# Differential attention with a gated feed-forward: branch-major order, and matmul work placed in pieces beside the scores

## The chip, the cores and the metric

One core of one Trainium2 chip runs the whole layer as one program. The metric is the device time in microseconds of an execution; smaller is better.

## The reference, cut to what matters

```python
x = L0_attn_x                       # (1, 1024, 256) float32
xn = layernorm(x)                   # no scale, no bias
# attention: 16 heads, two branches of queries and keys with 8 columns each, one set of values with 16
q1, k1, q2, k2, v = split(xn @ Wqkv, [128, 256, 384, 512])
lam = exp(lambda_q1 . lambda_k1) - exp(lambda_q2 . lambda_k2) + LAMBDA_INIT
A1 = causal_softmax(q1 k1^T / sqrt(8)) v
A2 = causal_softmax(q2 k2^T / sqrt(8)) v
diff = A1 - lam * A2
diff = (1 - LAMBDA_INIT) * diff / sqrt(mean(diff^2) + 1e-5)      # over the 16 columns of a head
attn = concat_heads(diff) @ Wproj
# feed-forward in fp8: 256 -> 2 x 1024 -> 256
ffn = (gelu(xn @ w_gating[0]) * (xn @ w_gating[1])) @ w_linear   # operands rounded to e4m3
out = x + attn + ffn
```

## The kernel before, in words

The program is written engine by engine, and each engine's list of instructions is its order; semaphores join them. There is no planner: the order of TensorE's work around the attention is written out by hand.

**Sizes.** 1024 tokens are eight blocks of 128 (TB). A group is four heads (J) of one branch; there are eight groups, and group g is heads g // 2 in branch g % 2, so the branches alternate. The causal scores of a head are cut into nine chunks of up to 512 columns (`CHUNKS`, line 42: key block, number of query blocks, first query); four heads times nine chunks are 36 items. A unit is three items, three of the eight PSUM banks: 12 units per group, 96 in all. Banks 0 to 2 and 3 to 5 hold the scores in turn; banks 6 and 7 collect the values' product, one for each half of the queries.

**Prefix.** VectorE normalizes x, TensorE transposes it (line 569), ScalarE copies it out. Eight units of queries and keys (line 584; `QK_UNITS` gives part and half, branch 1 is the first four) each go through ScalarE (high part, line 337) and VectorE (rest, line 419); SyncE spreads them by DMA over the partitions, eight DMAs for the stack of a group (line 228; four stacks fit, a later group's is loaded when an earlier group's scores are done). POOL squares the high parts (line 292). TensorE then projects the values (line 591), sums the squares into norms (line 603), makes 16 up products of the feed-forward (line 619), each followed by gelu on ScalarE (line 351) and the product with the second half on VectorE (line 436), and the down product (line 627), which VectorE copies out (line 445). From the norms VectorE works out a bound (line 368): a flag says whether exponentials could overflow without the row maxima, and a shift is the bias of the exponential. SyncE, VectorE and TensorE read the flag and run one of two bodies. With these inputs it is the one without row maxima.

**Attention.** Step n of the loop of TensorE (line 709) issues the scores of unit n (line 673), which wait for the exponential of unit n - 2, and then the values' product of the chunks that are due (line 695): chunk c of group g in step 12 g + last_unit(c) + `LAG`, with LAG = 3. ScalarE makes one exponential of 1536 columns per unit (line 360). POOL sets the part above the diagonal to zero in five of the nine chunks (line 319). The probabilities lie in a ring of six chunks (`KEPT`). When a half of the queries is complete, VectorE transposes it out of its bank (line 491), divides by the row sums (line 498), and after branch 2 of the same heads takes the difference, its mean square (lines 502 to 507), a root by bit shift and three Newton steps (lines 524 to 529; for the last heads by ScalarE's square root) and scales (line 511). A transpose back (line 544 or 549) makes the operand of the output projection (line 704), to which VectorE adds x and the feed-forward (line 556). Five DMAs write the output.

## Time and profile before

| what | value |
| --- | --- |
| median of 3 runs | 215.93 us (214.27 to 216.73) |
| the profiled execution | 216.52 us |
| its span | 214.7 us |
| busy: TensorE / ScalarE / VectorE / POOL | 181.4 / 162.7 / 92.2 / 62.3 us |
| granted TensorE clock, mean over the span | 0.971 |
| first exponential | 58.84 us |
| DMA, moved in all | 14.97 MB |

How to read it: the span is from the first to the last instruction of the profiled execution, and the execution's own time is 1.8 us longer. Busy time is a sum over the span; the stages have different limits, so what counts in each is which wait ends last. "PE" is TensorE (PEld its weight loads), "ACT" ScalarE, "DVE" VectorE, "POOL" GpSimd, "SP" SyncE. A clock of 1.00 is 2.4 GHz and 0.50 is 1.2 GHz. In the rows a time stands first (start in us), then the length in us, then engine, line, operation, output and input, and the count; brackets show how long the engine had idled and what ended that.

### The profile page before, as it was taken

What the parts mean: (1) busy time and instruction counts of PE and PEld (TensorE: products, weight loads), DVE (VectorE), ACT (ScalarE), POOL (GpSimd) and SP (SyncE); (2) the same over time, 40 slices, a digit from 0 to 9 for tenths busy, and PEclk for the clock granted to TensorE, in tenths of its full rate; (3) what the DMA queues carried; (4) which work ended last, traced back from release to release, by engine and by line L of the source; (5) the groups of instructions that cost most, each with busy time, mean ns of one, the idle gap of its engine ahead of it and who ended that gap; (6) DMA issues with size and microseconds to landing.
All of it is one profiled execution on the core that took longest, in us unless ns stands there. A gap on an engine that the chain in (4) does not pass through costs nothing.

```text
span 214.7 us, 3429 instructions
## 1 busy us (share of the span) xinstructions
PE 181.4 (84%) x1419; PEld 79.2 (37%) x1420; DVE 92.2 (43%) x182; ACT 162.7 (76%) x141; POOL 62.3 (29%) x71
## 2 busy tenths in 40 slices
PE   7699999997959988888888988888888888889970
PEld 7444485445722323322322332332232322232550
DVE  2835489885400004013961210992400595205581
ACT  2214334775096899999999999999999999999400
POOL 8306682000644203402601520440440350250000
PEclk9999999999975799999999999999999999999997
DMA  6965558840000034016007006100000000000014
GB/s 210 399 214 158 143 149 197 194 105 0 3 5 0 3 82 114 3 40 157 0 8 186 8 0 155 44 0 0 3 0 0 5 0 0 3 0 3 0 62 140
DMA packets 8149, 14.97 MB, mean 70 GB/s; under 512 B 1985, under 2 KB 5313, under 8 KB 8129
## 3 DMA queue, kind: packets, MB, share of 16 engines
q1 hardware_dynamic: 7584, 14.18, 24.0%
q10 hardware_dynamic: 544, 0.52, 0.7%
q8 instruction: 13, 0.21, 0.4%
q14 instruction: 8, 0.06, 0.1%
HBM read 5.26 MB, written 1.05 MB: 29 GB/s over the span
## 4 chain that ended last, share of the span: by engine, by line
ACT 62%; PE 29%; DVE 4%; DMA 2%; issue 1%; DVEq 0%; ACTq 0%
ACT probs L360 61%; PE ps L584 7%; PE ps L619 6%; PE ps L627 3%; PE ps L591 3%; PE ps L695 3%; PE ps L704 2%; PE ps L673 2%; DMA x_sb<-L_attn_x 2%; PE ps L569 1%; PE ps L603 1%; DVE stats L393 1%; DVE area L491 0%; DVE squares L544 0%; DVE area L436 0%
## 5 line engine op out<-in xcount | busy, mean ns | idle before, releaser
L360 ACT ACTIVATE probs<-ps,shift 128x1536 f32<-128x1536 f32 x96 | 137.9, 1853 | 10.0 <-PE ps L673 10.0
L695 PE MATMUL ps<-probs,v_all 128*32 128x512 f32 (+3 forms) x768 | 79.4, 510 | 0.4 <-ACT probs L360 0.4
L673 PE MATMUL ps<-q_st,k_st 32*128 32x512 f32 (+3 forms) x384 | 51.2, 432 | 21.3 <-ACT probs L360 20.9
L319 POOL TENSOR_SCALAR_AFFINE_SELECT probs<-probs 128x1024 f32<-128x1024 f32 (+1 forms) x40 | 38.0, 951 | 95.4 <-ACT probs L360 95.4
L673 PEld LDWEIGHTS ps<-q_st,k_st 32*128 32x128 f32 x384 | 23.4, 189 | 82.1 <-ACT probs L360 70.5
L491 DVE STREAM_TRANSPOSE area<-ps 128x512 f32<-128x512 f32 x16 | 11.4, 714 | 92.2 <-PE ps L695 92.1
L695 PEld LDWEIGHTS ps<-probs,v_all 128*32 128x32 f32 x768 | 17.2, 110 | 19.1 <-issue 13.7
L584 PE MATMUL ps<-xn_t,probs 128*128 128x512 f32 x32 | 15.9, 655 | 0.8 <-ACT xn_t L331 0.8
L619 PE MATMUL ps<-area 128*128 128x512 fp8e4 x64 | 14.1, 379 | 0.0
L292 POOL TENSOR_TENSOR squares<-parts 128x512 bf16<-128x512 f32 x8 | 8.3, 1042 | 12.9 <-ACT parts L337 12.9
L351 ACT ACTIVATE probs<-ps 128x512 bf16<-128x512 f32 x16 | 9.3, 597 | 3.3 <-PE ps L619 3.2
L436 DVE TENSOR_TENSOR area<-ps,probs 128x512 fp8e4<-128x512 f32 x16 | 10.8, 690 | 2.2 <-ACT probs L351 2.2
L307 POOL TENSOR_TENSOR x_sb<-x_sb,ffn 128x512 f32<-128x512 f32 x4 | 4.6, 1152 | 21.7 <-DVE ffn L445 21.7
L337 ACT ACTIVATE parts<-ps 128x512 fp32r<-128x512 f32 x8 | 4.8, 598 | 6.9 <-PE ps L584 6.7
L584 PEld LDWEIGHTS ps<-xn_t,probs 128*128 128x128 f32 x32 | 6.4, 207 | 8.4 <-issue 8.2
L619 PEld LDWEIGHTS ps<-area 128*128 128x128 fp8e4 x64 | 6.1, 98 | 7.7 <-DVE area L436 1.1
L498 DVE TENSOR_TENSOR area<-area,r_sum 128x512 f32<-128x512 f32 (+1 forms) x10 | 8.6, 858 | 0.3
L627 PE MATMUL ps<-area 128*128 128x256 fp8e4 x64 | 7.1, 272 | 1.5 <-DVE area L436 1.5
L704 PE MATMUL ps<-w_p,squares 128*128 128x256 f32 x32 | 7.4, 386 | 0.9 <-DVE squares L544 0.9
L419 DVE TENSOR_TENSOR parts<-ps,parts 128x512 fp32r<-128x512 f32 x8 | 5.5, 691 | 6.1 <-ACT parts L337 6.1
L331 ACT ACTIVATE xn_t<-ps 128x512 f32<-128x512 f32 x4 | 2.2, 595 | 7.4 <-PE ps L569 7.4
L591 PE MATMUL ps<-probs,xn_t 128*128 128x256 f32 x32 | 7.2, 379 | 0.0
(70 smaller groups left out, 113.5 us busy)
## 6 DMA issues: line engine op xcount, KB each, us to landing
q_st<-parts SPq DMA_DIRECT2D x32, 128.0 KB, 2.7
k_st<-parts SPq DMA_DIRECT2D x32, 128.0 KB, 2.7
probs<-L_ffn_w_gating SPq DMA_DIRECT2D x4, 512.0 KB, 8.4
probs<-L_ffn_w_linear SPq DMA_DIRECT2D x1, 1024.0 KB, 12.5
probs<-L_attn_Wqkv SPq DMA_DIRECT2D x2, 384.0 KB, 6.1
out<-probs SPq DMA_DIRECT2D x3, 256.0 KB, 2.9
x_sb<-L_attn_x ACTq DMA_DIRECT2D x2, 256.0 KB, 4.1
x_sb<-L_attn_x SPq DMA_DIRECT2D x2, 256.0 KB, 3.9
```

Source lines behind the costliest of these rows:

```text
L319: pool.affine_select(out=blocks, in_=blocks, pattern=pattern, compare_op=ALU.is_ge, fill=0.0, base=0, channel_multiplier=-1).then_inc(mask ...
L351: act.activation(gated[:, n % RING, :], ps[:, 2 * PAIR[n], :], ACT.Gelu_apprx_tanh).then_inc(gelu_ready, 1)
L360: act.activation(probs[:, at:at + PER_UNIT, :].rearrange("p s u -> p (s u)"), ps[:, 3 * (n % 2):3 * (n % 2) + 3, :].rearrange("p b n -> p ...
L436: dve.tensor_tensor(hidden[:, c, h * HALF:(h + 1) * HALF], ps[:, 2 * PAIR[n] + 1, :], gated[:, n % RING, :], ALU.mult, saturate=False).the ...
L491: dve.transpose(o_t[:, br, 16 * h:16 * h + 16, :].rearrange("p b w -> p (b w)"), ps[:, 6 + h, :]).then_inc(o_taken[h], 1)
L584: ins = pe.matmul(ps[:, (4 + u) % 8, :], w_q[:, k, i * P:(i + 1) * P], xn_t[:, k, h * HALF:(h + 1) * HALF], start=(k == 0), stop=(k == KC ...
L591: ins = pe.matmul(ps[:, 4 + b // 2, (b % 2) * C:(b % 2 + 1) * C], xn_t[:, k, b * P:(b + 1) * P], w_q[:, k, 2 * C:3 * C], start=(k == 0), s ...
L619: ins = pe.matmul(ps[:, 2 * PAIR[n] + g, :], w_gate8[:, g, k, c * P:(c + 1) * P], x8[:, k, h * HALF:(h + 1) * HALF], start=(k == 0), stop= ...
L627: ins = pe.matmul(ps[:, (6, 7, 4, 5)[b // 2], (b % 2) * C:(b % 2 + 1) * C], hidden[:, c, b * P:(b + 1) * P], w_lin8[:, c, :], start=(c == ...
L673: ins = pe.matmul(ps[:, bank, at:at + wide * P], k_st[rows, g % STACKS, kb * P:(kb + 1) * P], q_st[rows, g % STACKS, queries], start=True, ...
L695: ins = pe.matmul(ps[32 * j:32 * j + 32, 6 + half, q0 % HALF:q0 % HALF + wide * P], v_all[:, g // BR, kb, 32 * j:32 * j + 32], probs[:, sl ...
L704: ins = pe.matmul(ps[:, 4 + b // 2, (b % 2) * C:(b % 2 + 1) * C], out_t[:, p, b * P:(b + 1) * P], w_p[:, p, :], start=(p == 0 and b % 2 == ...
```

## The change

- **Order of the groups.** Groups 0 to 3 are branch 1 of all heads, 4 to 7 branch 2. The quotients of branch 1 are kept in a tile (`attn1`) until branch 2 of the same heads comes. Each branch has its own norms, bound, flag and shift. The loop over 96 units is cut in two bodies of 48; SyncE, VectorE and TensorE read a flag ahead of each.
- **Prefix.** TensorE makes only branch 1's four units of queries and keys, the first two value blocks and branch 1's norms (after the fourth up product), then the 16 up products. The casts of the gating weights go from VectorE to POOL, behind two of its squares. VectorE's reductions of the norms stand between its feed-forward products. The first scores wait for the 14th and 15th hidden tile instead of for the down product.
- **Beside the scores** (`beside(n)`, after the scores and values of unit n): value blocks 2 to 7 in units 0 to 5, branch 2's queries and keys in pieces in units 8 to 37, its four norms in units 23 to 41, and the down product in pieces in units 44 to 73. All of it but two value blocks goes through bank 7; VectorE alone copies the results out, between its own steps.
- **Values.** The product of both halves now uses bank 6 alone: the chunk list is in another order, in which the first half closes with the first piece of chunk 2, and the second half opens with its other piece one unit later, after VectorE has transposed the first half out (`o_taken`). The lag is 5 units instead of 3, 4 in group 6, and 3 or 2 in group 7.
- **Finish.** Each half of the queries is divided, and in branch 2 finished, by itself: `finish(i, h)` is a transpose, a division, the mean square, eleven root steps and the scaling. The copies of the down product, the residual sums on POOL and the transposes back stand between these steps. The output projection uses banks 0 to 3 at the end.

The diff, cut to its core:

```diff
 CHUNKS = [
-    [(0, 4, 0)], [(4, 4, 512)], [(3, 1, 384), (1, 3, 128)], [(7, 1, 896), (5, 3, 640)],
-    [(2, 2, 256), (6, 2, 768)], [(0, 4, 512)], [(1, 4, 512)], [(2, 4, 512)], [(3, 4, 512)],
+    [(0, 4, 0)], [(3, 1, 384), (1, 3, 128)], [(2, 2, 256), (6, 2, 768)], [(0, 4, 512)], [(4, 4, 512)],
+    [(1, 4, 512)], [(7, 1, 896), (5, 3, 640)], [(2, 4, 512)], [(3, 4, 512)],
 ]
-DIAGONALS = [[0], [0], [0, 128], [0, 128], [0, 256]]
-OPENS = ((0, 0), (1, 0))
-CLOSES = ((4, 0), (8, 0))
+DIAGONALS = {0: [0], 1: [0, 128], 2: [0, 256], 4: [0], 6: [0, 128]}
...
+V_AT = {0: (2,), 1: (3,), 2: (4,), 3: (5,), 4: (6,), 5: (7,)}
+QK_AT = {8: (4, 0, 0, 256), 9: (4, 0, 256, 256), 13: (4, 1, 0, 512), 17: (5, 0, 0, 512), 20: (5, 1, 0, 256),
+         21: (5, 1, 256, 256), 25: (6, 0, 0, 512), 29: (6, 1, 0, 512), 32: (7, 0, 0, 256), 33: (7, 0, 256, 256),
+         37: (7, 1, 0, 512)}
+NORM_AT = {23: 0, 31: 1, 39: 2, 41: 3}
+DOWN_AT = {44: (0, 0, 4), 45: (0, 4, 8), 49: (1, 0, 8), 53: (2, 0, 8), 56: (3, 0, 4), 57: (3, 4, 8), 61: (4, 0, 8),
+           65: (5, 0, 8), 68: (6, 0, 4), 69: (6, 4, 8), 73: (7, 0, 8)}
...
+def due(g, c):
+    if g < GROUPS - 2:
+        late = 5
+    elif g < GROUPS - 1:
+        late = 4
+    else:
+        late = (3, 3, 3, 3, 3, 2, 2, 2, 2)[c]
+    return g * STEPS + last_unit(c) + late
...
+            def second(i):
+                sp.wait_ge(scores_ready, STEPS * (i + 1))
+                sp.wait_ge(low_ready, 8)
+                stack(HG + i)
...
+            square_of(0)
+            square_of(1)
+            pool.wait_ge(wg_in, 64)
+            for k in range(KC):
+                for g in range(2):
+                    pool.tensor_copy(w_gate8[:, g, k, :], w_gate[:, g, k, :], saturate=False).then_inc(w8_ready, 1)
+            square_of(2)
+            square_of(3)
...
+                for c in sorted(DIAGONALS):
+                    mask(g, c)
+                    if (g, c) in ((1, 2), (1, 6), (2, 6), (3, 2)):
+                        square_of(4 + ((1, 2), (1, 6), (2, 6), (3, 2)).index((g, c)))
+                    if (g, c) in ((4, 4), (5, 2), (5, 6), (6, 4)):
+                        residual(((4, 4), (5, 2), (5, 6), (6, 4)).index((g, c)))
...
+                if n in (4, 5):
+                    t = n - 4
+                    dve.wait_ge(norms_ready, t + 1)
+                    dve.tensor_reduce(norm_most[:, 0, 2 * t:2 * t + 1],
+                                      ps[:, 4 + 2 * t:6 + 2 * t, :].rearrange("p b n -> p (b n)"), AX_X, ALU.max
+                                      ).then_inc(norms_taken, 1)
+                if n == 7:
+                    dve.wait_ge(norms_taken, 2)
+                    bound(dve, own, 0)
...
+            def finish(i, h):
+                take(HG + i, h)
+                divide(HG + i, h)
+                own.step(mean_square(i, h))
+                inverse_root(slice(16 * h, 16 * h + 16))
+                scale_by_root(i, slice(16 * h, 16 * h + 16))
...
+            for b in (2, 4, 6):
+                values_in(b)
+            dve.wait_ge(lam_exp, 1)
+            own.step(dve.tensor_tensor(lam_w[:, 4:5], lam_w[:, 3:4], lam_w[:, 2:3], ALU.subtract))
+            own.step(dve.tensor_scalar(neg_lam[:, :], lam_w[:, 4:5], -LAMBDA_INIT, None, ALU.add))
+            keep(0, 0)
+            split(4)
+            keep(0, 1)
+            keep(1, 0)
+            split(5)
+            norm_round(0)
+            keep(1, 1)
+            split(6)
+            norm_round(1)
+            keep(2, 0)
+            split(7)
+            norm_round(2)
+            keep(2, 1)
+            norm_round(3)
+            dve.wait_ge(round_taken, 4)
+            own.step(dve.tensor_tensor(norm_most[:, 1, 0:1], norm_most[:, 1, 0:1], norm_most[:, 1, 2:3], ALU.max))
+            own.step(dve.tensor_tensor(norm_most[:, 1, 2:3], norm_most[:, 1, 1:2], norm_most[:, 1, 3:4], ALU.max))
+            bound(dve, own, 1)
+            keep(3, 0)
+            keep(3, 1)
+            dve.wait_ge(flag_ready, 2)
+            with dve.If(dve.value_load(flag[0:1, 1:2], min_val=0, max_val=1) == 1):
+                maxima(1)
+            down(0)
+            finish(0, 0)
+            down(1)
+            finish(0, 1)
+            down(2)
+            finish(1, 0)
+            down(3)
+            finish(1, 1)
+            turn_back(0, 0)
+            turn_back(0, 1)
+            finish(2, 0)
+            finish(2, 1)
+            finish(3, 0)
+            turn_back(1, 0)
+            take(GROUPS - 1, 1)
+            divide(GROUPS - 1, 1)
+            mean_square(3, 1).then_inc(ms_ready, 1)
+            dve.wait_ge(rms_ready, 1)
+            own.step(dve.reciprocal(root[:, 16:32], u[:, 16:32]))
+            scale_by_root(3, slice(16, 32))
...
+                if n == NORMS_AFTER:
+                    pe.wait_ge(picks_set, BR)
+                    pe.wait_ge(squared, 4)
+                    pe.wait_ge(hidden_ready, 2)
+                    for u in (0, 2, 1, 3):
+                        ins = norms(u, 4 + 2 * (u % 2) + u // 2)
+                        if u >= 2:
+                            ins.then_inc(norms_ready, 1)
+                pe.wait_ge(x8_ready, h + 1)
                 if n < 2:
-                    pe.wait_ge(v_out, TB // 2 * (n + 1))
-                elif n < 4:
-                    pe.wait_ge(bound_ready, 1)
-                else:
+                    pe.wait_ge(low_ready, 2 * n + 2)
+                elif n == 2:
+                    pe.wait_ge(v_out, 2)
+                elif n >= NORMS_AFTER:
                     pe.wait_ge(hidden_ready, max(m for m in range(n) if PAIR[m] == PAIR[n]) + 1)
+                if n == 6:
+                    pe.wait_ge(norms_taken, 1)
+                if n == 7:
+                    pe.wait_ge(norms_taken, 2)
...
+            def beside(n):
+                for b in V_AT.get(n, ()):
+                    if n == 0:
+                        pe.wait_ge(hidden_ready, len(FFN))
+                    if b >= 6:
+                        pe.wait_ge(v_out, 4)
+                    project_values(b, 7 - (b // 2 + 1) % 2)
+                if n in QK_AT:
+                    u, k, at, wide = QK_AT[n]
+                    if n == min(QK_AT):
+                        pe.wait_ge(v_out, TB)
+                    elif (k, at) == (0, 0):
+                        pe.wait_ge(low_ready, u)
+                        if u >= 6:
+                            pe.wait_ge(round_taken, u - 5)
+                    ins = queries_keys(u, 7, k, at, wide)
+                    if k == KC - 1 and at + wide == HALF:
+                        ins.then_inc(qk_ready, 1)
+                if n in NORM_AT:
+                    r = NORM_AT[n]
+                    pe.wait_ge(squared, 4 + r + 1)
+                    pe.wait_ge(low_ready, (6, 7, 8, 8)[r])
+                    if r == 3:
+                        pe.wait_ge(round_taken, r)
+                    norms(4 + r, 7).then_inc(round_ready, 1)
+                if n in DOWN_AT:
+                    b, first, end = DOWN_AT[n]
+                    if n == min(DOWN_AT):
+                        pe.wait_ge(wl8_ready, 1)
+                        pe.wait_ge(round_taken, 4)
+                    if b >= 2 and b % 2 == 0 and first == 0:
+                        pe.wait_ge(ffn_out, b // 2)
+                    for c in range(first, end):
+                        ins = pe.matmul(ps[:, 7, (b % 2) * C:(b % 2 + 1) * C], hidden[:, c, b * P:(b + 1) * P],
+                                        w_lin8[:, c, :], start=(c == 0), stop=(c == HC - 1))
+                    if end == HC and b % 2 == 1:
+                        ins.then_inc(down_ready, 1)
...
+                (kb, wide, q0), *more = CHUNKS[c]
+                if g == 0 and c < 2:
+                    pe.wait_ge(v_out, (6, TB)[c])
+                if c == 0 and g > 0:
+                    pe.wait_ge(o_taken, 2 * g)
+                ins = product(g, c, 0, kb, wide, q0, c == 0)
+                if c in (MIXED, LAST):
+                    ins.then_inc(o_ready, 1)
+                elif more:
+                    product(g, c, wide * P, *more[0], False)
+            def second_half(g):
+                first, (kb, wide, q0) = CHUNKS[MIXED]
+                pe.wait_ge(o_taken, 2 * g + 1)
+                product(g, MIXED, first[1] * P, kb, wide, q0, True)
...
+                for n in range(n0, n0 + BRANCH if br == 0 else UNITS + 3):
                     if n < UNITS:
                         scores(n, general)
-                    for c in range(NC):
-                        g, u = divmod(n - LAG - last_unit(c), STEPS)
-                        if u == 0 and 0 <= g < GROUPS:
-                            values(g, c)
-                pe.wait_ge(wp_in, 16 * 8)
-                pe.wait_ge(out_t_ready, 1)
-                project(0, 0)
-                for h in range(2):
-                    pe.wait_ge(o_taken[h], GROUPS)
-                project(1, 0)
-                for h in range(2):
-                    pe.wait_ge(out_t_ready, h + 2)
-                    project(h, 1)
+                    values_due(n, HG if general and br == 1 else 0, GROUPS)
+                    beside(n)
+            pe.wait_ge(wl8_ready, 1)
             pe.wait_ge(flag_ready, 1)
-            too_large = pe.value_load(flag[0:1, 0:1], min_val=0, max_val=1)
-            with pe.If(too_large == 0):
-                attention(False)
-            with pe.If(too_large == 1):
-                row_maxima()
-                attention(True)
+            large1 = pe.value_load(flag[0:1, 0:1], min_val=0, max_val=1)
+            with pe.If(large1 == 0):
+                attention(0, False)
+            with pe.If(large1 == 1):
+                attention(0, True)
+            pe.wait_ge(flag_ready, 2)
+            large2 = pe.value_load(flag[0:1, 1:2], min_val=0, max_val=1)
+            with pe.If(large2 == 0):
+                attention(1, False)
+            with pe.If(large2 == 1):
+                attention(1, True)
+            pe.wait_ge(exp_done, UNITS)
+            pe.wait_ge(wp_in, 16 * 8)
+            pe.wait_ge(out_t_ready, 3)
+            project(0, 0)
+            project(0, 1)
+            project(1, 0)
+            pe.wait_ge(out_t_ready, 4)
+            project(1, 1)
```

## Rows read from the trace of the kernel before

**Rows 1.** The page, costliest groups (busy, mean ns, idle before) and DMA issues

```profile
L360 ACT ACTIVATE probs<-ps,shift 128x1536 f32<-128x1536 f32 x96 | 137.9, 1853 | 10.0 <-PE ps L673 10.0
...
L673 PE MATMUL ps<-q_st,k_st 32*128 32x512 f32 (+3 forms) x384 | 51.2, 432 | 21.3 <-ACT probs L360 20.9
...
q_st<-parts SPq DMA_DIRECT2D x32, 128.0 KB, 2.7
```

**Rows 2.** ScalarE in time, steady part (start us, us, what, idle before)

```profile
72.13 38.77 ACT L360 ACTIVATE probs<-ps,shift 128x1536 f32<-128x1536 f32 x27 [1.04 <-PE ps L673]
```

**Rows 3.** TensorE in time, from the start to the first exponential

```profile
14.91 12.18 PE L584 MATMUL ps<-xn_t,probs 128*128 128x512 f32 x28
...
35.56 14.08 PE L619 MATMUL ps<-area 128*128 128x512 fp8e4 x64
51.15 7.15 PE L627 MATMUL ps<-area 128*128 128x256 fp8e4 x64 [1.50 <-DVE area L436]
```

**Rows 4.** ScalarE in time, before and at the first exponentials

```profile
50.30 1.28 ACT L354 ACT_TABLE_LOAD   x1
...
58.84 7.27 ACT L360 ACTIVATE probs<-ps,shift 128x1536 f32<-128x1536 f32 x5 [7.05 <-PE ps L673]
```

**Rows 5.** TensorE in time, the end

```profile
199.72 1.06 PE L695 MATMUL ps<-probs,v_all 128*32 128x512 f32 x8 [0.36 <-ACT probs L360]
...
205.37 3.72 PE L704 MATMUL ps<-w_p,squares 128*128 128x256 f32 x16 [0.94 <-DVE squares L544]
```

**Rows 6.** TensorE in time, one steady unit

```profile
78.11 0.50 PE L673 MATMUL ps<-q_st,k_st 32*128 32x512 f32 x3 [1.01 <-ACT probs L360]
78.54 1.07 PE L695 MATMUL ps<-probs,v_all 128*32 128x512 f32 x8
```

**Rows 7.** POOL in time, from the start

```profile
16.77 2.05 POOL L292 TENSOR_TENSOR squares<-parts 128x512 bf16<-128x512 f32 x2 [9.12 <-ACT parts L337]
...
28.79 2.36 POOL L296 CAST area<-probs 128x2048 fp8e4<-128x2048 f32 x1
```

**Rows 8.** VectorE in time, beside the up products

```profile
35.30 1.23 DVE L372 TENSOR_REDUCE norm_most<-ps 128x1 f32<-128x1024 f32 x1
...
37.86 0.17 DVE L384 TENSOR_SCALAR shift<-shift 128x8 f32<-128x8 f32 x1
38.36 3.14 DVE L436 TENSOR_TENSOR area<-ps,probs 128x512 fp8e4<-128x512 f32 x5 [0.33 <-ACT probs L351]
```

**Rows 9.** SyncE in time, one of the stacks' issues

```profile
24.11 0.60 SPq L232 DMA_DIRECT2D q_st<-parts  x1
```

**Rows 10.** Windows: busy us (count) of each engine, granted clock, DMA share, GB/s

```profile
60.00:62.00 2.00, 0.69 (x7) 0.43 (x10) 0.00 (x0) 2.00 (x3) 0.37 (x2) 1.00 0.01 4
...
58.80:72.00 13.20, 10.43 (x68) 3.79 (x68) 0.23 (x1) 10.35 (x7) 5.48 (x6) 0.63 0.01 2
...
88.00:104.00 16.00, 13.40 (x130) 4.39 (x128) 4.74 (x6) 16.00 (x12) 4.97 (x5) 1.00 0.28 67
```

**Rows 11.** TensorE's weight loads in time, at the first scores

```profile
58.23 0.19 PEld L673 LDWEIGHTS ps<-q_st,k_st 32*128 32x128 f32 x3 [0.21 <-issue]
```

**Rows 12.** POOL in time, a mask of two blocks

```profile
139.60 1.10 POOL L319 TENSOR_SCALAR_AFFINE_SELECT probs<-probs 128x1024 f32<-128x1024 f32 x1 [1.37 <-ACT probs L360]
```

**Rows 13.** VectorE in time, finishing the last halves

```profile
195.21 0.72 DVE L491 STREAM_TRANSPOSE area<-ps 128x512 f32<-128x512 f32 x1 [8.00 <-PE ps L695]
...
196.71 0.48 DVE L502 SCALAR_TENSOR_TENSOR area<-area,neg_lam 128x256 f32<-128x256 f32 x1
...
198.14 0.17 DVE L507 TENSOR_SCALAR newton<-newton 128x16 f32<-128x16 f32 x1
```

**Rows 14.** VectorE in time, small steps of an earlier finish

```profile
139.75 0.99 DVE L524 TENSOR_SCALAR halved<-newton 128x32 int32<-128x32 int32 x1
...
142.22 0.19 DVE L529 SCALAR_TENSOR_TENSOR newton<-newton 128x32 f32<-128x32 f32 x1
...
143.58 0.19 DVE L529 SCALAR_TENSOR_TENSOR newton<-newton 128x32 f32<-128x32 f32 x1
```

564 lines of the change are left out of this document (286 added, 278 removed).

## The prediction

> **What bounds the kernel now.** I read the costliest groups first. The 96 exponentials are 137.9 us of ScalarE, and it idled 10.0 us before them; TensorE idled 21.3 us before the scores, nearly all of it waiting for an exponential [rows 1]. Then the timelines: from 72.13 us on 27 exponentials end to end take 38.77 us, 1.436 each [rows 2], and 96 x 1.436 = 137.9. So ScalarE sets the pace of the attention once it runs. Before it lies a serial part: TensorE goes through the projections, the up products and the down product (51.15 to 58.30) without a real gap [rows 3], and the first exponential starts at 58.84 after 7.05 us of idling [rows 4]. The span is therefore 58.84 us of prefix, 137.9 of exponentials, 3.0 of holes between them (10.0 - 7.05) and 15.0 from the last exponential's end (199.7, where the last product starts [rows 5]) to 214.7. The reader should see in the steady unit that TensorE needs 0.43 for scores and 1.00 for a chunk of values [rows 6], 1.43 against ScalarE's 1.436: its only slack is the 3 units in 12 that have no chunk, 20.9/8 = 2.6 us per group [rows 1].
>
> **Prefix.** TensorE before ended eight query/key units at 27.1; a piece is 12.18/28 = 0.43 and a unit has four [rows 3]. After, four units go (-6.9) and two value blocks of four pieces with half the columns, 0.22, come in (+1.8): projections end at 22.0. The weights' casts go from VectorE to POOL, behind two squares. Those started at 16.77 [rows 7]; the second transposes now stand one unit later (+1.7), so 18.5 to 20.5; four casts of 1024 at 2.36/2 = 1.18 [rows 7] end at 25.2. TensorE idles 3.2 us for them. Up products: four take 3.5 (14.08/64 = 0.22 a matmul [rows 3]), norms 0.9, the fifth 0.9: 30.5. From an up product's end to its hidden tile took 1.5 before (49.64 to 51.15 [rows 3]); I use 1.3 inside the stream: 31.8. Now VectorE is the link: reduction 1.23 [rows 8], product 0.63 (3.14/5 [rows 8]), reduction 1.23: 34.9. Up product 8 waits for the second reduction, as its banks hold the norms: 35.8, hidden 37.1, the bound 1.5 (36.53 to 38.03 [rows 8]): 38.6. Then products 9 to 12, 2.5 us, with two lambda dots at the 0.17 of a small step: 41.4; the last up product needs that bank: 42.3. Its gelu ends near 43.0, table load 1.28 [rows 4] and the lambda exponential follow: first exponential at 44.6, **14.2 us earlier**. Stacks of branch 1 are issued from 23.4, eight issues of 0.6 with their gaps, 5 us each [rows 9]; the first is there at 31, no wait. Ends: casts in VectorE's shadow or a slower link give 13 to 16.
>
> **The first six units.** Before, TensorE was busy 0.69 of 2 us here, and the granted clock averages 0.63 from 58.8 to 72.0, so some 9.8 us of that were at 0.50, which is 1.2 GHz [rows 10]; those made the 3.0 us of holes. After, a value block (0.9) fills each of units 0 to 5, so I take the 3.0 as gone; ends 0 and 3.
>
> **What the slots hold.** Query/key work of branch 2 is four units of 1.72 in slots 8, 9, 13 ... 37: 0.43, 0.43, 0.86, 0.86, 2.6 per group, against 2.6 of slack. The down product, 64 x 0.11 = 7.15 [rows 3], in slots 44 to 73 gives 2.7 per group. That adds nothing while nothing waits, but leaves no slack: a TensorE wait is absorbed up to 0.9 us (1.436 less the scores of 0.5), once, and after that goes straight to ScalarE. For four norm matmuls and shape switches I add 1.0 us in all (0 to 3: at the top end the 30-odd added pieces each pay 0.1, half a weight load of 0.19 [rows 11]).
>
> **The waits.** *Unit 41:* its norm needs the last square, which stands on POOL behind the mask of chunk 2: 1.10 [rows 12] and 1.04 [rows 7] from the unit's start, plus 0.25: over a unit by 1.0. It eats the 0.9, 0.1 is lost. From here to 73 TensorE is saturated.
>
> *Unit 48:* one branch body ends, TensorE jumps over the other (all of attention with row maxima) and reads a second flag. The nearest row is the first flag, 0.21 of weight-load idle [rows 11]; the far end is a DMA landing, 2.7 [rows 1]. I take 1.0, nearer to the flag since the values of unit 47 cover a microsecond. The Trainium skill (Runtime: NRT & Kernel Launch, Instruction fetch mechanics) says that a taken branch to a target outside the prefetched window waits for a fetch; no row shows one. By it the sum would be 2 us higher.
>
> *Unit 53:* the down product waits for its bank, which VectorE copies out only after it has taken and divided the half that unit 52 ends: 1.50 (195.21 to 196.71, three operations [rows 13]), a flag read of 0.2 (the first flag's on TensorE), a copy as long as a take, 0.7, against 0.45 of scores: 2.0 lost. Queued behind it are all later scores.
>
> *Finishing a half.* VectorE must transpose and divide (1.50), take the mean square (196.71 to 198.31, 1.60 [rows 13]), do eleven small steps at 0.226 (seven from 142.22 to 143.80 [rows 14]) and scale (0.45): 6.05. One step per half will meet a POOL mask: a small one took 0.99 at 139.75 instead of 0.18, while a mask ran from 139.60 [rows 12]. So 6.5, four and a half units. Before nobody waited for it; now the second half of chunk 2 shares bank 6 and waits for the transpose, and the down product for bank 7. Then: unit 61 waits for copy 2 of the down product, 6.5 + 0.75 against 6.65 of TensorE work: 0.6. Unit 68 waits for copy 3, behind the half that unit 64 ends: 7.25 against 5.25: 2.0. Unit 80 waits for a transpose that stands behind the half of unit 76 and two transposes back, as long as a take's 0.72 [rows 13]: 6.5 + 1.5 + 0.75 = 8.7 against 4.8: 3.8, of which 0.4 free in slot 80 and the part won in 79 are absorbed: 2.9. Unit 91, behind the half of unit 87: 7.25 against 4.75: 2.5, with the double chunk of unit 93 behind it, 2.1 lost. Together 7.6; without collisions 5.5, and with two each 10.
>
> **End.** The last chunk ends 1.1 after the last exponential as before. Three projections of 1.86 (3.72/2 [rows 5]) run beside VectorE's finishing, 1.50 + 1.60 + root, scale and turn 1.7 = 4.8, then the fourth: 1.1 + 7.4 = 8.5 against 9.4 before; the 5.6 behind stays. 14.2 against 15.0.
>
> **Sum.** Span 44.6 + 137.9 + (0.1 + 1.0 + 2.0 + 7.6 + 1.0 = 11.7) + 14.2 = 208.4, against 214.7. The profiled execution took 216.5, 1.8 more than its span: 210.2. The median of the runs is 0.6 lower, 215.9: **209.5**.
>
> **Rivals.** *A, the waits are cheap* (VectorE gets through a half in 5.5 or the jump is free): the losses are 5 instead of 11.7, 203. For it: small steps on 16 instead of 32 columns; against: their length hardly depends on columns (0.17 to 0.19 [rows 13, 14]). *B, one fall of the clock.* TensorE idles 3.2 at 22.0, about 2 near 33, 3.8 in unit 80. Before, a stretch at low load was followed by about 10 us at 1.2 GHz [rows 10]. With every slot filled, half of such a stretch is lost: 8 us cost 4, 213.5. *C, slower.* The same in at least two places, the up products and units 80 to 91: 16 us at 1.2 GHz lose 8, 217.5; it decides from 13 us at 1.2 GHz on (half of it is the 6.5 us that I forecast as gain). Against B and C: the steady units run at clock 1.00 although TensorE idles a sixth there [rows 10]. *D, the jump is a fetch*: the landing's 2.7 [rows 1] plus about 1 for the flag and restart, 3.7 instead of my 1.0: 212. It rests on the rule of the Trainium skill named at unit 48. The slots' numbers say that the moved work itself is hidden; were it not, TensorE would need 17.2 + 1 us per group, 6 us more over six groups: that is the upper end of the forecast with the shape switches.
>
> **Chances.** Forecast (206.5 to 213) 0.50, A 0.20, B 0.14, C 0.10, D 0.06. The range 202 to 214 leaves out C, half of B and a tail of A and of the forecast. About 1% is what a measurement tells from no change: faster is the forecast, A, D and half of B with a little taken off for the upper tail, 0.80; within 1% 0.11; slower 0.09.
>
> **What would show it.** First exponential at 44.6 (43 to 46), TensorE idle for the casts from 22. ScalarE idle before exponentials beyond the first about 11 to 12 us, with the largest holes at units 80 and 91 and below 1 us in units 1 to 40. VectorE 6 to 6.5 us per half in branch 2. Clock 1.00 in the first ten units. Wrong if holes stand in the first forty units (then the slots don't fit), if a stretch at 1.2 GHz shows, or if the first exponential is later than 47.

## The result, and the profile after

The changed kernel takes **235.88 us** (median of 4 runs, 235.4 to 237.01) against 215.94 us of the kernel before on the same chip: ratio 1.094, interval 1.087 to 1.102. It is slower by 20 us, where 209.5 was forecast and 202 to 214 given. The profiled execution took 235.4 us with a span of 233.7. A ratio with an interval, here and below, compares on both sides only executions within 1.5% of their kernel's quickest one, so it can differ from the ratio of the medians.

I cut each span at the first exponential's start and the last one's end (us):

| kernel | to the first | exponentials | behind the last | span |
| --- | --- | --- | --- | --- |
| before | 58.8 | 140.8 | 15.0 | 214.7 |
| forecast | 44.6 | 149.6 | 14.2 | 208.4 |
| after | 46.1 | 171.9 | 15.7 | 233.7 |

The prefix gave 12.7 us, as the change meant it to; the 96 exponentials take 31 us longer. The rows of the page that answer to [rows 1], with the granted clock in 40 slices:

```profile
PEclk9999799999999999999975876999799858988978
...
L421 ACT ACTIVATE probs<-ps,shift 128x1536 f32<-128x1536 f32 x96 | 141.8, 1540 | 30.0 <-PE ps L843 29.2
L855 PE MATMUL ps<-probs,v_all 128*32 128x512 f32 (+3 forms) x768 | 86.7, 543 | 9.0 <-DVE o_t L553 7.8
...
L843 PE MATMUL ps<-q_st,k_st 32*128 32x512 f32 (+3 forms) x384 | 53.3, 450 | 3.7 <-issue 3.4
```

ScalarE idled 30.0 us for scores instead of 10.0 (of which 7.05 stood ahead of the first exponential), and TensorE, which used to wait 21.3 us for exponentials, no longer does: its waits are for VectorE and for "issue". The clock falls in several slices of the second half. Where, ScalarE's timeline shows (start, length, count, in brackets the idle time before):

```profile
46.10 35.62 ACT L421 ACTIVATE probs<-ps,shift 128x1536 f32<-128x1536 f32 x24
...
106.35 11.90 ACT L421 ACTIVATE probs<-ps,shift 128x1536 f32<-128x1536 f32 x8 [0.21 <-PE ps L843]
121.93 1.54 ACT L421 ACTIVATE probs<-ps,shift 128x1536 f32<-128x1536 f32 x1 [3.68 <-PE ps L843]
124.57 1.54 ACT L421 ACTIVATE probs<-ps,shift 128x1536 f32<-128x1536 f32 x1 [1.10 <-PE ps L843]
...
129.82 4.56 ACT L421 ACTIVATE probs<-ps,shift 128x1536 f32<-128x1536 f32 x3 [1.04 <-PE ps L843]
137.72 1.54 ACT L421 ACTIVATE probs<-ps,shift 128x1536 f32<-128x1536 f32 x1 [3.34 <-PE ps L843]
...
165.67 1.54 ACT L421 ACTIVATE probs<-ps,shift 128x1536 f32<-128x1536 f32 x1 [2.68 <-PE ps L843]
...
188.85 1.54 ACT L421 ACTIVATE probs<-ps,shift 128x1536 f32<-128x1536 f32 x1 [4.23 <-PE ps L843]
191.45 1.54 ACT L421 ACTIVATE probs<-ps,shift 128x1536 f32<-128x1536 f32 x1 [1.06 <-PE ps L843]
...
210.41 1.54 ACT L421 ACTIVATE probs<-ps,shift 128x1536 f32<-128x1536 f32 x1 [2.90 <-PE ps L843]
```

A hole is idle time of ScalarE between two exponentials. Five large ones (3.68, 3.34, 2.68, 4.23, 2.90) belong to waits of TensorE at units 48, 53, 68, 80 and 91, all of them places where the prediction had put a loss. (The last four waits stand behind the scores of their unit, so ScalarE misses the scores of the next one, 54, 69, 81 and 92; the text goes by TensorE's unit.) Behind them come single exponentials with 0.4 to 1.2 us between them. TensorE's timeline says what they are:

```profile
116.58 1.07 PE L855 MATMUL ps<-probs,v_all 128*32 128x512 f32 x8
121.03 0.80 PE L843 MATMUL ps<-q_st,k_st 32*128 32x512 f32 x3 [3.38 <-issue]
121.76 1.93 PE L855 MATMUL ps<-probs,v_all 128*32 128x512 f32 x8
...
135.90 1.05 PE L796 MATMUL ps<-area 128*128 128x256 fp8e4 x8 [3.11 <-DVE ffn L614]
```

Unit 48 starts after 3.38 us in which TensorE waited for nothing that the profile shows, and at this place it jumps over the body with row maxima. Behind it the same scores take 0.80 instead of 0.50 and the same chunk 1.93 instead of 1.07. The windows (TensorE busy first, granted clock in the third column from the end) show the clock:

```profile
118.00:120.00 2.00, 0.00 (x0) 0.00 (x0) 0.00 (x0) 0.25 (x1) 0.00 (x0) 0.96 0.42 94
120.00:122.00 2.00, 0.97 (x7) 0.52 (x11) 0.00 (x0) 0.07 (x1) 0.00 (x0) 0.50 0.83 203
...
128.00:130.00 2.00, 2.00 (x18) 0.70 (x14) 0.00 (x0) 0.95 (x2) 1.10 (x1) 0.50 0.43 102
130.00:132.00 2.00, 2.00 (x19) 0.35 (x11) 0.00 (x0) 1.95 (x2) 0.57 (x1) 0.98 0.00 0
```

After the idle 118 to 121 the clock is at 0.50 (1.2 GHz) until about 130, while TensorE is busy without a gap. A unit that needs 1.43 us of TensorE [rows 6] then needs 2.7, ScalarE still 1.436: 1.1 to 1.2 us are lost per unit.

**Ledger.** The exponentials lose 34.0 us over 96 x 1.436 = 137.9 (forecast 11.7). The holes of 48, 53, 61, 68, 80, 91 (the one at 61 a small one): 3.7 + 3.3 + 0.4 + 2.7 + 4.2 + 2.9 = 17.3 (forecast 10.6). Slow units behind them, by how much each stretch from a hole's end to the return of the 1.436 pace is over that pace: 3.8 + 3.0 + 1.0 + 2.8 + 1.8 = 12.4 (forecast none for the clock). About 0.9 of the last 1.8 is not the clock's: TensorE makes the two chunks of unit 93 in 1.92 us at a granted clock of 1.00 (212 to 214), and the same 0.75 us of idling stands there in experiment 5, whose waits are filled. So some 11.5 us are units at 1.2 GHz. The first 48 units, which end at 118.25: 72.15 - 68.9 = 3.2 (forecast 1.1 for these and the rest together). The remainder 1.1.

### The profile page after: what moved, and what is told of

Its sections match the earlier page's. It is cut to its first block, busy times and chain, and to the rows that moved or that the text cites. A ratio compares the mean times of both kernels' runs of the same rounds, so it can differ in the third digit from the quotient of the medians.

```text
span 233.7 us, 3560 instructions
## 1 busy us (share of the span) xinstructions
PE 198.9 (85%) x1426; PEld 80.8 (35%) x1426; DVE 104.4 (45%) x273; ACT 162.1 (69%) x130; POOL 63.2 (27%) x75
## 4 chain that ended last, share of the span: by engine, by line
PE 63%; DVE 17%; ACT 9%; issue 4%; POOL 4%; DMA 1%; DVEq 1%
PE ps L855 25%; PE ps L843 14%; ACT probs L421 8%; PE ps L758 6%; PE ps L705 6%; PE ps L884 4%; PE ps L796 3%; PE ps L711 3%; DVE o_t L553 2%; POOL area L342 2%; DMA x_sb<-L_attn_x 1%; DVE newton L580 1%; POOL squares L334 1%; DVE newton L579 1%; PE ps L695 1%
## 5 line engine op out<-in xcount | busy, mean ns | idle before, releaser
L421 ACT ACTIVATE probs<-ps,shift 128x1536 f32<-128x1536 f32 x96 | 141.8, 1540 | 30.0 <-PE ps L843 29.2
L855 PE MATMUL ps<-probs,v_all 128*32 128x512 f32 (+3 forms) x768 | 86.7, 543 | 9.0 <-DVE o_t L553 7.8
L553 DVE STREAM_TRANSPOSE o_t<-ps 128x512 f32<-128x512 f32 x16 | 11.4, 713 | 67.1 <-PE ps L855 67.0
L705 PE MATMUL ps<-xn_t,w_q 128*128 128x512 f32 (+1 forms) x38 | 19.0, 612 | 0.8 <-ACT xn_t L389 0.8
L796 PE MATMUL ps<-area 128*128 128x256 fp8e4 x64 | 10.4, 306 | 5.5 <-DVE ffn L614 5.5
L758 PEld LDWEIGHTS ps<-area 128*128 128x128 fp8e4 x64 | 6.3, 103 | 15.4 <-issue 6.3
L705 PEld LDWEIGHTS ps<-xn_t,w_q 128*128 128x128 f32 x38 | 7.0, 210 | 8.7 <-issue 8.7
L796 PEld LDWEIGHTS ps<-area 128*128 128x128 fp8e4 x64 | 5.8, 105 | 11.0 <-DVE ffn L614 6.6
L711 PE MATMUL ps<-w_q,xn_t 128*128 128x256 f32 x32 | 8.7, 399 | 1.0 <-DVE area L482 1.0
L605 DVE CAST parts<-ps 128x512 fp32r<-128x512 f32 x4 | 2.8, 692 | 14.2 <-PE ps L705 14.2
L884 PEld LDWEIGHTS ps<-w_p,squares 128*128 128x128 f32 x32 | 7.2, 227 | 4.6 <-issue 3.4
```

Source lines behind the costliest of these rows:

```text
L421: act.activation(probs[:, at:at + PER_UNIT, :].rearrange("p s u -> p (s u)"), ps[:, 3 * (n % 2):3 * (n % 2) + 3, :].rearrange("p b n -> p ...
L553: dve.transpose(o_t[:, h, :, :].rearrange("p b w -> p (b w)"), ps[:, 6, :]).then_inc(o_taken, 1)
L705: return pe.matmul(ps[:, bank, at:at + wide], w_q[:, k, i * P:(i + 1) * P], xn_t[:, k, h * HALF + at:h * HALF + at + wide], start=(k == 0 ...
L711: ins = pe.matmul(ps[:, bank, (b % 2) * C:(b % 2 + 1) * C], xn_t[:, k, b * P:(b + 1) * P], w_q[:, k, 2 * C:3 * C], start=(k == 0), stop=(k ...
L758: ins = pe.matmul(ps[:, 2 * PAIR[n] + g, :], w_gate8[:, g, k, c * P:(c + 1) * P], x8[:, k, h * HALF:(h + 1) * HALF], start=(k == 0), stop= ...
L796: ins = pe.matmul(ps[:, 7, (b % 2) * C:(b % 2 + 1) * C], hidden[:, c, b * P:(b + 1) * P], w_lin8[:, c, :], start=(c == 0), stop=(c == HC - 1))
```

## The experiments

The running theory after the comparison: (1) a jump over a long body costs TensorE 3.4 to 4 us wherever it stands; (2) VectorE's order (a whole finish ahead of each copy or transpose that TensorE waits for) makes the other holes; (3) each such wait is followed by units at 1.2 GHz, which cost about as much again. Its rivals are that the holes come from the traffic of the DMAs or from the moved work itself; the slow units are slow for their own reasons. All kernels were run beside the kernel before (medians of 215.6, 216.3, 213.9 and 216.7 us in the four series); ratios are to that. The prefix varies between executions: the first eight pieces of projection take 3.67 us in some and 5.4 to 6.2 in others, so stages are compared from the first exponential on.

**1. No bodies, no flags.** The diff, of `after`, on TensorE (VectorE and SyncE likewise):

```diff
-            pe.wait_ge(flag_ready, 1)
-            large1 = pe.value_load(flag[0:1, 0:1], min_val=0, max_val=1)
-            with pe.If(large1 == 0):
-                attention(0, False)
-            with pe.If(large1 == 1):
-                attention(0, True)
...
+            attention(0, False)
+            attention(1, False)
```

> The changed kernel without the bodies for row maxima and without the flag reads on TensorE, VectorE and SyncE (that guard is left out); every other instruction stays. Theory (the jump is a fetch, then a fall of the clock): the hole of 3.7 us at unit 48 and the 3.3 us of slow units behind it go, the hole at unit 53 loses the 1.2 us of VectorE's flag read, and the 2.5 us ahead of the output projection go with its slow stretch: 10 to 12 us less than the changed kernel, 224 to 226. Rival (the slots are overfull, the jump only shows a lag that was there): under 3 us less, 233 or more, and ScalarE stands at unit 48 as before.

Measured 220.73 us (216.39 to 223.21), span 214.7. ScalarE's timeline:

```profile
102.23 20.58 ACT L398 ACTIVATE probs<-ps,shift 128x1536 f32<-128x1536 f32 x14 [0.21 <-PE ps L813]
125.83 1.54 ACT L398 ACTIVATE probs<-ps,shift 128x1536 f32<-128x1536 f32 x1 [3.02 <-PE ps L813]
```

Fourteen exponentials run through unit 48 without a hole; the holes at 53, 68, 80 and 91 stay (3.02, 2.39, 4.22, 2.19). The exponentials take 161.1 us instead of 171.9, the end 11.6 instead of 15.7. It came out below its expectation of 224 to 226. In the profiled execution 4.1 us of that are an earlier first exponential, by the quick start (3.67 us for the eight pieces). The rest is in the slow units, whose number varies: TensorE's wait at unit 80 is 4.25 us as before, but only 0.8 us are lost behind it instead of 2.8, and 0.3 instead of 3.0 behind unit 53 (2.8 instead of 1.0 behind 68, 2.5 instead of 1.8 behind 91):

```profile
176.02 1.54 ACT L398 ACTIVATE probs<-ps,shift 128x1536 f32<-128x1536 f32 x1 [4.22 <-PE ps L813]
178.25 14.45 ACT L398 ACTIVATE probs<-ps,shift 128x1536 f32<-128x1536 f32 x10 [0.69 <-PE ps L813]
```

The hole and the slow units at 48 are gone and the other large holes are not. So the jump and the waits are two separate causes.

**2. VectorE's order alone.** In place of a finish in one piece, each half's transpose and division go first, and the copy or transpose that TensorE waits for goes ahead of the root:

```diff
-            down(0)
-            finish(0, 0)
+            keep2(0, 0)
+            own.step(mean_square(0, 0))
             down(1)
-            finish(0, 1)
+            root_of(0, 0)
+            keep2(0, 1)
             down(2)
-            finish(1, 0)
+            own.step(mean_square(0, 1))
+            take(HG + 1, 0)
+            root_of(0, 1)
+            divide(HG + 1, 0)
...
```

Also the first down copy now goes ahead of `keep(3, 1)`, and the later groups follow the same pattern.

> The changed kernel with another order of VectorE's steps in branch 2: each take and each copy of the down product stands ahead of the root steps of the half before; jumps stay on TensorE. Theory (VectorE's order makes the holes at units 53, 61, 68, 80, 91, and each is followed by units at 1.2 GHz): holes of 13.5 us and some 7.5 us of slow units go, 214 to 218; the hole and slow units at unit 48 stay. Rival (TensorE has too much work, holes only move): less than 8 us gained, 228 or more, holes before exponentials spread over all units.

Measured 212.41 us (median of 12 runs, 207.92 to 215.69; 0.985 of the median before), ratio 0.971 (0.962 to 0.979), a little less than expected; span 213.6. ScalarE:

```profile
122.96 1.54 ACT L421 ACTIVATE probs<-ps,shift 128x1536 f32<-128x1536 f32 x1 [3.99 <-PE ps L872]
...
130.84 39.68 ACT L421 ACTIVATE probs<-ps,shift 128x1536 f32<-128x1536 f32 x27 [1.04 <-PE ps L872]
```

Only the group at unit 48 is left; from there on not one hole above 0.5. The exponentials take 150.6. Twenty-one of the 34 us were VectorE's order and its clock falls, with all the moved work still in its slots: the moved work itself isn't the main loss.

**3. Order and nested flags.** TensorE's second flag is read inside the first body, so that the far jump comes only behind its last instruction; and the last square goes one mask earlier.

```diff
             with pe.If(large1 == 0):
                 attention(0, False)
+                second(0)      # reads flag 2, branch 2 and the projections inside
             with pe.If(large1 == 1):
                 attention(0, True)
-            pe.wait_ge(flag_ready, 2)
-            large2 = pe.value_load(flag[0:1, 1:2], min_val=0, max_val=1)
...
+                second(1)
```

> Both, with nothing left out: VectorE's new order, TensorE's second flag read inside the body of the first so that no jump is taken until the end, and the last square one mask earlier. Theory: what is left is 46 to first exponential, 137.9 for the exponentials, 4 to 6 us of units over 1.436 and 14 to 15 at the end: 203 to 208, faster than the kernel before. Rival (overfull slots, or the clock falls anyway in a TensorE that is never idle): 215 or more.

Measured 206.67 us (204.68 to 208.08), ratio 0.961 (0.941 to 0.980), span 204.0. ScalarE:

```profile
46.18 35.60 ACT L421 ACTIVATE probs<-ps,shift 128x1536 f32<-128x1536 f32 x24
...
106.37 54.95 ACT L421 ACTIVATE probs<-ps,shift 128x1536 f32<-128x1536 f32 x38 [0.21 <-PE ps L872]
```

All 96 in 142.1 us, 4.2 over 137.9. This is what the slots cost when nothing waits long; the forecast for it was 1.0, with 3 as its upper end.

**4. The jump in the kernel before.** Its loop is cut behind unit 47 into two bodies, nothing else:

```diff
-                attention(False)
+                attention(False, 0)
             with pe.If(too_large == 1):
                 row_maxima()
-                attention(True)
+                attention(True, 0)
+            too_large2 = pe.value_load(flag[0:1, 0:1], min_val=0, max_val=1)
+            with pe.If(too_large2 == 0):
+                attention(False, 1)
+            with pe.If(too_large2 == 1):
+                attention(True, 1)
```

> The kernel before with one thing done: TensorE's loop of 96 units is cut after unit 47 in two bodies, each behind a flag read, so TensorE jumps once over the other body. Theory: a hole of 2.8 to 3.7 us at unit 48 and then slow units at 1.2 GHz, which cost 2 to 3 more: 219 to 223. Rival (a jump costs what the first flag showed, 0.2 us, or is hidden by the values' products): 216 to 217.

Measured 220.46 us, ratio 1.027 (1.015 to 1.039). TensorE, then ScalarE:

```profile
130.08 0.80 PE L673 MATMUL ps<-q_st,k_st 32*128 32x512 f32 x3 [4.00 <-issue]
130.81 1.94 PE L695 MATMUL ps<-probs,v_all 128*32 128x512 f32 x8
```

```profile
130.92 1.54 ACT L360 ACTIVATE probs<-ps,shift 128x1536 f32<-128x1536 f32 x1 [2.53 <-PE ps L673]
...
138.92 2.97 ACT L360 ACTIVATE probs<-ps,shift 128x1536 f32<-128x1536 f32 x2 [1.17 <-PE ps L673]
142.15 61.88 ACT L360 ACTIVATE probs<-ps,shift 128x1536 f32<-128x1536 f32 x43 [0.25 <-PE ps L673]
```

The jump alone, without any other part of the change, makes the same hole and the same slow units behind it: 2.5 us and then 1.06 + 1.15 + 1.17 on ScalarE, 4.9 us in the median. The slack that the kernel before has at this place did not shelter it.

**5. Work in the waits of `after`.** Small products of the identity, whose result nobody reads, run ahead of the waits at 53, 68, 80 and 91 (6, 4, 16, 10 of them); the waits stay:

```diff
+            def warm(n, count):
+                if count:
+                    pe.wait_ge(exp_done, n)
+                for _ in range(count):
+                    pe.matmul(ps[:, 3 * ((n + 1) % 2), 0:P], ident[:, :], ident[:, :], start=True, stop=True)
```

> The changed kernel with only matmuls of the identity added, into score banks that are free, while TensorE stands at the waits of units 53 (6), 68 (4), 80 (16) and 91 (10). The waits stay. Theory (a good part of the loss is the clock that falls in the waits): the slow units behind units 80 and 91, 2.5 and 1.5 us, and part of those behind 53 and 68, go: 4 to 7 us less than the changed kernel's 235.9, 229 to 232. Rival (the waits alone cost, slow units are a symptom of something else): 235 or more, since added work can only delay.

Measured 226.84 us (225.84 to 228.13), ratio 1.050 (1.044 to 1.057): 9 us less than `after` by doing more, and 2 us less than the expectation's lower end. ScalarE:

```profile
121.51 1.54 ACT L421 ACTIVATE probs<-ps,shift 128x1536 f32<-128x1536 f32 x1 [3.83 <-PE ps L844]
124.15 1.54 ACT L421 ACTIVATE probs<-ps,shift 128x1536 f32<-128x1536 f32 x1 [1.09 <-PE ps L844]
...
137.03 11.92 ACT L421 ACTIVATE probs<-ps,shift 128x1536 f32<-128x1536 f32 x8 [3.05 <-PE ps L844]
...
161.64 13.20 ACT L421 ACTIVATE probs<-ps,shift 128x1536 f32<-128x1536 f32 x9 [2.10 <-PE ps L844]
...
183.24 15.88 ACT L421 ACTIVATE probs<-ps,shift 128x1536 f32<-128x1536 f32 x11 [3.54 <-PE ps L844]
```

The filled holes are 0.3 to 0.7 us smaller (3.05, 2.10, 3.54 and 2.22 for 3.34, 2.68, 4.23 and 2.90), since the first matmuls behind the wait are quick too, and behind three of them eight, nine and eleven exponentials follow without a gap, while behind the unfilled jump at 121.51 the slow units stay. So the slow units belong to the idle time of TensorE and not to the work behind it. This is the experiment in which the run times show it: the slowest execution is 7 us below the quickest of `after`.

**6 and 7. One wait by itself.** In the version of experiment 3 TensorE waits once, ahead of unit 37, for a chain of memsets on POOL that nobody needs; the second kernel runs 14 small products during that wait:

```diff
+                if n == 37:
+                    for _ in range(14):        # 0 in experiment 6
+                        pe.matmul(ps[:, 3, 0:P], ident[:, :], ident[:, :], start=True, stop=True)
+                    pe.wait_ge(gap, 1)
```

> The reordered kernel (third experiment) with one wait added: ahead of unit 37's scores TensorE waits for a chain of POOL memsets that starts with unit 36's scores and takes some 4 us. Theory: a hole of 2 to 3.5 us in ScalarE and behind it two to four units of 2.6 instead of 1.43 us, 3 us more: 5 to 7 us above the reordered kernel, 211.5 to 213.5. Rival: the hole alone, 2 to 3.5 us, 209 to 210.

> The same wait at the same place, but TensorE runs 14 small matmuls of the identity (3.1 us) during it. Theory: the hole stays, the slow units don't come: 2 to 3.5 us above the reordered kernel, 209 to 210, some 3 us less than with the idle wait. Rival: as the idle wait.

Measured 211.24 us (span 209.4) and 209.45 (span 207.4; ratio 0.968, 0.961 to 0.974), against 206.67. ScalarE in the one and in the other:

```profile
105.24 1.54 ACT L428 ACTIVATE probs<-ps,shift 128x1536 f32<-128x1536 f32 x1 [3.71 <-PE ps L883]
108.08 1.54 ACT L428 ACTIVATE probs<-ps,shift 128x1536 f32<-128x1536 f32 x1 [1.30 <-PE ps L883]
110.20 1.54 ACT L428 ACTIVATE probs<-ps,shift 128x1536 f32<-128x1536 f32 x1 [0.58 <-PE ps L883]
111.95 54.96 ACT L428 ACTIVATE probs<-ps,shift 128x1536 f32<-128x1536 f32 x38 [0.21 <-PE ps L883]
```

```profile
105.32 4.52 ACT L428 ACTIVATE probs<-ps,shift 128x1536 f32<-128x1536 f32 x3 [3.25 <-PE ps L883]
110.06 54.97 ACT L428 ACTIVATE probs<-ps,shift 128x1536 f32<-128x1536 f32 x38 [0.21 <-PE ps L883]
```

A wait of 3.36 us on TensorE costs 5.6 us of ScalarE's idle time (7.9 in all against 2.3 in experiment 3), the same wait kept busy 3.3 (5.6 against 2.3). One fall of the clock is worth 2.3 us between these two traces. The run times don't show it: the medians differ by 1.8 us, but the runs overlap (207.63 to 213.79, 208.17 to 211.59), and the quickest of all is one with the idle wait. The size rests on one execution of each.

**8. The casts ahead of the squares.** On top of experiment 3:

```diff
-            square_of(0)
-            square_of(1)
             pool.wait_ge(wg_in, 64)
...
+            square_of(0)
+            square_of(1)
             square_of(2)
```

> The reordered kernel with POOL's four casts of the gating weights ahead of its first two squares instead of behind. Theory (TensorE's 3.0 us of idling at 22 us is the casts' place in POOL's queue): the up products start when the projections end, the first exponential comes 3 to 4 us earlier (42 to 43), and 1.4 us of slow up products can't come: 202 to 204. Rival (the weights land only after 20 us, or the squares then hold up the norms): less than 1 us gained.

Measured 202.59 us (201.0 to 203.48), ratio 0.937 (0.930 to 0.944), span 200.0. POOL and TensorE:

```profile
13.55 3.99 POOL L340 CAST area<-probs 128x1024 fp8e4<-128x1024 f32 x4 [5.91 <-DMA probs<-L_ffn_w_gating]
```

```profile
23.30 2.75 PE L787 MATMUL ps<-area 128*128 128x512 fp8e4 x12 [0.64 <-DVE parts L470]
```

The casts start as soon as the weights have landed, in 1.0 us each instead of the 1.18 from [rows 7], and end at 17.5 instead of 24.7. TensorE's 3.02 us of waiting for them is gone, and so is the slow stretch behind it: in `after` sixteen up matmuls took 5.03, here the same sixteen 1.03 + 2.75. The wait doesn't bring the slow stretch each time, though: in experiments 1 and 9, which started quickly, TensorE waited 3.03 and 3.02 us for the casts too, and the sixteen behind took 3.63. The first exponential comes at 42.3 with the same slow start as in `after` (5.60 for the eight pieces). This version computes everything and is the quickest of those.

**9. The body's length.** `after` with the flag reads and the branches kept, only TensorE's bodies with row maxima shortened:

```diff
             with pe.If(large2 == 1):
-                attention(1, True)
+                pe.matmul(ps[:, 3, 0:P], ident[:, :], ident[:, :], start=True, stop=True)
```

> The changed kernel with TensorE's two bodies for row maxima shrunk to one small matmul each (that path is left out); both flag reads and both branches stay, on VectorE and SyncE as well. It tells a far jump from a branch. Theory (what costs is the fetch behind a far jump): the hole at unit 48 shrinks from 3.7 us to under 1, no slow units follow it, and the 2.5 us ahead of the output projection go: 222 to 227. Rival (the flag's load into a register and the branch cost it): the holes stay, 234 to 237.

Measured 223.24 us (220.46 to 227.1), ratio 1.048 (1.037 to 1.059). TensorE at unit 48:

```profile
112.49 1.06 PE L855 MATMUL ps<-probs,v_all 128*32 128x512 f32 x8
113.49 0.50 PE L843 MATMUL ps<-q_st,k_st 32*128 32x512 f32 x3
```

Unit 47's values run straight into unit 48's scores: the flag read and the branch cost TensorE nothing that can be seen, the distance costs 3.4 us. The stacks of branch 2 are loaded at the same time in both kernels, so the rival of the DMAs' traffic falls (their share is 0.80 from 118 to 120 here, where nothing waits, and 0.42 in `after`, where TensorE stands). The exponentials take 165.2, the end 11.5. Against experiment 1, which has VectorE's flag read taken out too, TensorE waits 3.11 instead of 1.96 at unit 53, from the same point: VectorE's flag read is worth 1.15 on TensorE.

**10 and 11. The far jump behind the last product.** The same shortening in the kernel before, and in the version of experiment 8. Both leave out the body with row maxima.

> The kernel before, with TensorE's two bodies for the row-maxima path (never entered here) shrunk to one small matmul each; the flag reads and the branches stay, so only the distance that the branch jumps over differs. Theory that a branch over a long body costs wherever it stands, also as TensorE's last instruction at the end of the kernel: the end of the kernel before, from VectorE's last add to the end of the span (5.6 us against 3.3 to 3.4 in the versions whose last jump isn't TensorE's last instruction), shrinks by some 2 us: 213.5 us against 215.5. Rival, that a jump behind the last matmul holds up nobody: no change, 215.5 us, and the 5.6 us stay.

> The version with the changed order of VectorE, TensorE's nested flag reads and the gating casts ahead of the squares (202.6 us), with TensorE's two bodies for the row-maxima path (never entered here) shrunk to one small matmul each. If the length of the body that is jumped over still costs at the end alone: 2 to 3.7 us less, about 199.5 us, all of it behind the last exponential (15.5 us there before, 12 to 13.5 here). Rival, no cost left in it: 202.6 us, the same exponentials' span of 142 us and the same end.

Measured 212.91 us (ratio 0.979, 0.974 to 0.983) and **198.18 us** (198.06 to 198.27; ratio 0.915, 0.912 to 0.917). SyncE's waits in experiments 8 and 11:

```profile
SPq L121 <- DMA out<-probs: 4.9, 1, 4.9
```

```profile
SPq L121 <- DMA out<-probs: 1.5, 1, 1.5
```

The stage of the exponentials is unchanged (142.1 us in both, 140.8 in experiment 10 as in the kernel before). The end shrinks from 15.5 to 11.9 and from 15.0 to 12.7; in the kernel before SyncE's last wait goes from 3.6 to 1.5, the rest of experiment 10's gain (0.85) is an earlier first exponential. So the kernel before, too, pays about 2.2 us for a jump behind its last matmul, and the version of experiment 8 pays 3.6: nothing waits for TensorE then, but the program ends later. In `after`, whose far jump stands ahead of the projections, this last wait is 1.5 as well; nesting the flags had moved the cost to the end. I had put that in the unchanged "5.6 behind". Which event the last wait is really held up by, the traces don't show.

## Why the prediction was wrong, step by step

- **Prefix, 14.2 gained:** 12.7. The casts were waited for 3.02 us, as said (3.2), but the sixteen up matmuls behind took 5.03 instead of 3.5 at a clock that had fallen (0.57 to 0.58 from 24 to 28). Experiment 8 removes both; in experiments 1 and 9 the wait came without the fall.
- **First units:** the holes of before are gone; that step holds. But the 48 units lose 3.2 instead of 1.1. The term that was mis-sized is the piece in a slot. A whole piece of queries and keys takes 1.06 us to the next scores, where 0.86 was taken, a half piece 0.63 for 0.43, a value block 1.06 for 0.9:

```profile
65.09 1.13 PE L705 MATMUL ps<-xn_t,w_q 128*128 128x512 f32 x2
66.15 0.55 PE L843 MATMUL ps<-q_st,k_st 32*128 32x128 f32 x6
```

  With a value block a unit is 1.49 to 1.55, with a half piece 1.68, and the first 24 exponentials take 35.62 instead of 34.46; holes of 0.2 to 0.3 stand at units 24, 32 and 40, behind the norms of 23, 31 and 39. All 96 lose 4.2 where nothing waits long (experiment 3), above the 3 that I had called the upper end.
- **Unit 48, the step that failed first:** taken as 1.0, measured 3.7 plus 3.8 of slow units. I took the nearer row, a flag read, because a microsecond of values covered it, and left the fetch to a rival with 0.06. The rival's size, 3.7, is what came, but it was put together from a DMA's landing and a guess, so that the figure fits is luck. The Trainium skill (Runtime: NRT & Kernel Launch, Instruction fetch mechanics) says that a taken branch beyond the prefetched pages must wait for a fetch; the runs agree: 3.38, 3.69 and 4.00 us of "issue" where the body is long (after, experiments 2 and 4), none where it is short (9). The page gives no price. That the time is a fetch no trace shows; what the runs show is that it hangs on the length of the body.
- **Unit 53:** 3.3 for 2.0. VectorE's flag read was taken as 0.2 from TensorE's; its row shows 1.20:

```profile
133.53 0.42 DVE L560 TENSOR_TENSOR attn<-o_t,r_sum 128x256 f32<-128x256 f32 x1
135.15 0.69 DVE L614 CAST ffn<-ps 128x512 bf16<-128x512 f32 x1 [1.20 <-issue]
```

- **Finishing a half:** 6.5 forecast; 6.5, 6.5, 7.6, 7.1, 6.7, 7.0 and 5.9 measured. Two collisions with POOL instead of one in some, as here on VectorE and POOL:

```profile
167.38 1.02 DVE L579 SCALAR_TENSOR_TENSOR newton<-newton 128x16 f32<-128x16 f32 x1
168.44 1.10 DVE L580 TENSOR_TENSOR newton<-newton 128x16 f32<-128x16 f32 x1
```

```profile
167.28 1.10 POOL L364 TENSOR_SCALAR_AFFINE_SELECT probs<-probs 128x1024 f32<-128x1024 f32 x1 [6.46 <-ACT probs L421]
168.35 1.16 POOL L370 TENSOR_TENSOR x_sb<-x_sb,ffn 128x512 f32<-128x512 f32 x1
```

- **Units 61, 68, 80, 91:** 0.4, 2.7, 4.2, 2.9 against 0.6, 2.0, 2.9, 2.1. Where and why was right. TensorE's waits were 1.99, 4.25 and 3.03 at 68, 80 and 91 for 2.0, 3.8 and 2.5 forecast, the two longer ones by the longer halves. At 80 and 91 TensorE did have a lead of 0.9, but the first values and scores behind the wait ran at 1.2 GHz and took 0.8 more, so that the wait of 4.25 stood on ScalarE as 4.23; at 48, 53 and 68 it had no lead. By the first matmuls behind all five waits I estimate that 2.7 of the holes' 17.3 us are the clock's in this way; experiment 5, which fills four of them, got 2.2 back.
- **The clock, the step that decides:** I forecast none of it (rivals B and C together 0.24) and gave as the reason that steady units run at 1.00 though TensorE idles a sixth there. That row [rows 10] speaks of many short pauses, not of one of 3 us. Behind five waits the slow units cost 11.5 us, and some 2.7 more lie in the holes. How many slow units follow a wait is not told by its length alone (4.25 us were followed by 2.8 us of loss here, by 0.8 in experiment 1); what else decides stays open. C had the mechanism and the sign; it priced two places at 8 us where there were five, and didn't add the fetch, as I had made rivals of mechanisms that simply add up.
- **End:** 14.2 forecast, 15.7 measured. The 32 matmuls of the projections ran in one piece, without the pause of [rows 5], but began 2.47 us after the last chunk, behind another far jump, and took 8.83 instead of 7.17 us; with the short body there is no gap, and the end is 11.5 (experiment 9). The 14.2 held a cost of the kernel before that I hadn't seen: 2.2 of the "5.6 behind" are its own far jump (experiment 10).

Sum: 208.4 + 1.5 (prefix) + 6.7 (holes) + 12.4 (slow units, 11.5 of it the clock) + 3.2 (full slots, remainder) + 1.5 (end) = 233.7. Three sums of the forecast are not exact: 6.5 + 1.5 + 0.75 less 4.8 at unit 80 is 3.95 and not 3.8, the end's 8.5 + 5.6 is 14.1, and a fetch at unit 48 is put at 2 us more in one place and at 2.7 in rival D. None of them turns anything.

Of the signs that I had named for being wrong, two came: holes within the first forty units, small ones, and stretches at 1.2 GHz. The clock of 1.00 in the first ten units came too.

The idea of the change was sound: with the order on VectorE, on POOL and of the branches put right, the same rearrangement takes 202.6 us, 6.3% less than before, and 198.2 without the long body.

## What to carry to other kernels

When work is moved into an engine's slack, list first every wait that this slack used to shelter: here five waits of 2 to 4 us, four of them made by work that stood on VectorE ahead of the copy or transpose that TensorE needed, in three cases a whole finish. Where TensorE has no slack, price a wait of 2 to 4 us once for itself and once for the units at 1.2 GHz behind it (here 0.9 to 3.8 us in `after`, and as little as 0.3 in experiment 1), or put the copy ahead of the chain. Keep rarely taken bodies out of the straight path, or nest them so that the jump comes where nobody waits (at the end it still cost 3.6 us here), and don't let rivals that can happen together share one chance.
